# Down-weight quantization, low products and residual add moved in a fused cross-attention and FP4 feed-forward kernel

## The reference

```python
def fp4_quant_dequant(x):                 # along the last dim, blocks of 16
    scale = max(max(|xb|) / 6.0, 1e-12)
    q = GRID[searchsorted(MID, |xb / scale|)] * sign(xb) * scale
def fp4_linear(x, w):
    return einsum('bsk,nk->bsn', fp4_quant_dequant(x), fp4_quant_dequant(w))

x = x + autocorrelation_attention(layernorm(x), ctx, ctx, Wq, bq, Wout, bout)
h = silu(fp4_linear(layernorm(x), w_gate)) * fp4_linear(layernorm(x), w_up)   # 704 wide
x = x + fp4_linear(h, w_down)
```

## Time and profile before

| | |
|---|---|
| median of three executions | 526.64 us |
| profiled execution | 528.21 us, its span 526.4 us |
| busy, share of the span | TensorE 91%, VectorE 87%, ScalarE 74%, GpSimd 48% |
| mean granted TensorE clock | 0.964 |
| mean duration, split h (L533, L534, L536) | 1.2 to 1.3 us over all forms |
| largest_h (L1182), scaling_h (L1176) | 1620 ns, 1698 ns |
| ScalarE's copy of a weight fill, gate and up | four in 2.87 us |
| hqT transposes, issue to landing | 3.8 us median |

### The profile page before, as it was taken

One profiled execution on the slowest core, in us unless ns is written; L12 is line 12 of the kernel. 1 busy time (PEld: TensorE's weight loads), 2 busy tenths in 40 slices (PEclk: granted clock), 3 DMA queues, 4 the chain that ended last, 5 costly groups with the idle time before them and its releaser, 6 DMA issues.

```text
span 526.4 us, 10114 instructions
## 1 busy us (share of the span) xinstructions
PE 476.7 (91%) x3490; PEld 315.4 (60%) x3490; DVE 456.9 (87%) x762; ACT 391.9 (74%) x670; POOL 254.2 (48%) x326
## 2 busy tenths in 40 slices
PE   4599897858699999999999999999999999899957
PEld 4587787723355666666656666666666666466635
DVE  3789967598679999999999999999999999999981
ACT  3267875775978888888888788888888877766661
POOL 3225550256245566665655556666565558333330
PEclk9989997978899999999999999999999999899989
DMA  8988810432055676576675575656666564444636
GB/s 274 346 264 269 277 51 26 86 85 56 1 95 106 134 131 129 120 132 128 143 125 116 121 140 122 130 116 126 141 121 138 117 118 93 97 97 95 133 69 150
DMA packets 164723, 68.68 MB, mean 130 GB/s; under 512 B 129088, under 2 KB 164416, under 8 KB 164672
## 3 DMA queue, kind: packets, MB, share of 16 engines
q1 hardware_dynamic: 164672, 68.03, 57.3%
HBM read 27.38 MB, written 9.18 MB: 69 GB/s over the span
## 4 chain that ended last, share of the span: by engine, by line
issue 34%; POOL 21%; DVE 20%; PE 13%; ACT 5%; DMA 4%; SPq 1%; POOLq 1%; DVEq 1%; ACTq 0%
POOL ctx_sb L466 13%; POOL sl L482 6%; DVE w_q_lo L1144 4%; DVE ctx_sb L1097 3%; DVE y_h L1176 2%; DVE x_t L895 2%; PE ps L724 2%; ACT h_c L536 2%; PE ps L842 2%; ACT h_c L533 2%; PE ps L843 1%; DMA w_raw<-in_L_ffn_w_up_dram 1%; PE ps L704 1%; PE ps L844 1%; PE ps L714 1%
## 5 line engine op out<-in xcount | busy, mean ns | idle before, releaser
L842 PE MATMUL ps<-guT_hi,a_xT 128*128 128x512 f16 (+1 forms) x384 | 141.9, 370 | 14.1 <-DVE hb L1092 7.4
L843 PE MATMUL ps<-guT_lo,a_xT 128*128 128x512 f16 (+1 forms) x384 | 142.1, 370 | 0.0
L844 PE MATMUL ps<-guT_hi,a_xT 128*128 128x512 f16 (+1 forms) x384 | 141.6, 369 | 0.0
L852 PE MATMUL ps<-dT_hi,hqT 128*128 128x256 f16 x704 | 130.5, 274 | 7.6 <-ACT a_xT L594 5.7
L466 POOL TENSOR_TENSOR ctx_sb<-w_q_lo,sl 128x704 f16<-128x704 f16 x62 | 96.2, 1574 | 29.4 <-DVE ctx_sb L1097 29.3
L533 ACT ACTIVATE h_c<-y_h 128x1408 bf16<-128x1408 bf16 (+3 forms) x39 | 47.8, 1226 | 75.9 <-DVE y_h L1176 58.7
L854 PE MATMUL ps<-dT_lo,hqT 128*128 128x256 f16 x384 | 88.4, 275 | 0.0
L517 POOL TENSOR_TENSOR xs<-xs,w_raw 128x512 f32<-128x512 f32 x30 | 36.0, 1200 | 101.1 <-issue 101.1
L852 PEld LDWEIGHTS ps<-dT_hi,hqT 128*128 128x128 f16 x704 | 69.3, 98 | 18.7 <-issue 6.0
L842 PEld LDWEIGHTS ps<-guT_hi,a_xT 128*128 128x128 f16 x384 | 38.1, 99 | 62.5 <-issue 15.7
L844 PEld LDWEIGHTS ps<-guT_hi,a_xT 128*128 128x128 f16 x384 | 38.2, 100 | 40.5 <-issue 3.5
(11 more groups left out here) (161 smaller groups left out, 863.9 us busy)
## 6 DMA issues: line engine op xcount, KB each, us to landing
xs<-in_x_dram SPq DMA_DIRECT2D x16, 512.0 KB, 6.1
ctx_sb<-in_ctx_dram SPq DMA_DIRECT2D x16, 512.0 KB, 5.1
out_dram<-a_xT SPq DMA_DIRECT2D x64, 128.0 KB, 2.0
w_raw<-a_scratch SPq DMA_DIRECT2D x60, 128.5 KB, 2.7
hqT<-ctx_sb SPq DMA_TRANSPOSE x64, 3.8
w_raw<-in_L_ffn_w_down_dram SPq DMA_DIRECT2D x1, 704.0 KB, 6.3
w_raw<-in_L_ffn_w_gate_dram SPq DMA_DIRECT2D x1, 640.0 KB, 5.9
w_raw<-in_L_ffn_w_up_dram SPq DMA_DIRECT2D x1, 640.0 KB, 6.9
```

The source lines that it names most:

```text
L842: pe.matmul(dst, xt[:, c, :], guT[0][:, c, n0:n1], start=(c == 0), stop=False)
L843: pe.matmul(dst, xt[:, c, :], guT[1][:, c, n0:n1], start=False, stop=False)
L844: last = pe.matmul(dst, xt[:, KC + c, :], guT[0][:, c, n0:n1], start=False, stop=(c == KC - 1))
L852: pe.matmul(dst, hqT[:, j % 4, c, :], dT_hi[:, c, :], start=(c == 0), stop=False)
```

## The change

Four things are edited, in the order of the kernel:
- **Weights.** The load of the down weights goes ahead of the last two quads. `w_prepare(1)` runs in quad 14, its maximum is spread between the last correlations, scales and both segments follow the last evac_qk; both `w_finish` go between the softmax's sum and `wp`. ScalarE splits them before the exponential and evacuates all eight gate and up fills after it. The low part of the gate and up weights is written one quad later and waits for the next segment's w_finish. The transposes of the down weights go ahead of the filler products (28 in place of 20) and between tiles of pairs 0 and 1.
- **Stages 0 and 1.** In stage 0 ScalarE does silu(0) first; from stage 1 on (before, from stage 2) VectorE does the x steps among the h steps.
- **Low products.** GpSimd does low_scales ahead of low_h, and low_h waits for scaling_h (`yh_done`). Those of pairs 29 and 30 are done by VectorE, in one instruction each.
- **Residual.** L855 and ScalarE's copy go. VectorE computes bank x inv_out + xs for both tiles of a pair in one instruction, after products_x, and SP stores a pair at once. The last pair's tiles are done singly.
- **Drain** (st = NP): the order of VectorE's steps, and of SP's stores and transposes, is new.

```diff
@@ SP @@
             for i in range(2, NQ):
+                if i == NQ - 2:
+                    down_v = w_raw[:, 256 * GU_CH:WCOLS].rearrange("p (c n) -> p c n", n=FF)
+                    sp.dma_start(down_v, w_down.rearrange("(c p) n -> p c n", p=P)).then_inc(s["d_loaded"], 16)
                 load_x(i)
                 load_c(i)
...
-                    sp.wait_ge(s["loh"], i + 1)
+                    if i // 2 >= NP - 3:
+                        sp.wait_ge(s["z_lo"], i // 2 - NP + 4)
+                    else:
+                        sp.wait_ge(s["loh"], i + 1)
...
+            def store(q):
+                sp.wait_ge(s["o_done"], q + 1)
+                sp.dma_start(out[2 * q:2 * q + 2].rearrange("b l d -> l b d"), of[:, 2 * (q % 2):2 * (q % 2) + 2, :]
+                             ).then_inc(stored[q % 2], 16)
...
-                if tile_ok(2 * st - 8):
-                    store(2 * st - 8)
                 if pair_ok(st + 1):
                     turn_x(st + 1)
-                if tile_ok(2 * st - 7):
-                    store(2 * st - 7)
+                if pair_ok(st - 4) and st < NP:
+                    store(st - 4)
+                if st == NP + 1:
+                    store(NP - 4)
+                    turn_h(2 * NP - 2)
+                    store(NP - 3)
+                    turn_h(2 * NP - 1)
+                    store(NP - 2)
+                    store_last(0)
+                    store_last(1)
@@ GpSimd @@
             def w_lo(g):
                 pool.wait_ge(s["w_hi"], g + 1)
+                if g + 1 < N_GU:
+                    pool.wait_ge(s["w_steps"], finish_at(g + 1) + 3)
...
-                if turn(i - 2) is not None:
-                    w_lo(turn(i - 2))
+                if turn(i - 3) is not None:
+                    w_lo(turn(i - 3))
...
+            w_lo(N_GU)
+            w_lo(N_GU + 1)
...
             for st in range(FIRST, END):
                 if st == NP:
                     low_scales(NP - 1)
-                if pair_ok(st - 3) and st <= NP + 1:
-                    low_h(st - 3)
                 if 2 <= st < NP:
                     low_scales(st - 1)
+                if pair_ok(st - 3) and st < NP:
+                    pool.wait_ge(s["yh_done"], st - 1)
+                    low_h(st - 3)
@@ ScalarE @@
             keep_v(NQ // QT - 1)
-            evacuate_weights(act, range(EARLY))
+            w_split(N_GU)
+            w_split(N_GU + 1)
             act.wait_ge(s["t_steps"], 3)
             act.activation(wexp[:, :], corr[:, 0, 0:P], ACT.Exp, bias=nmx[:, 0:1]).then_inc(s["t_exp"], 1)
-            evacuate_weights(act, range(EARLY, GU_FILLS))
-            w_split(N_GU)
-            w_split(N_GU + 1)
+            evacuate_weights(act, range(GU_FILLS))
+            w_hi(N_GU)
+            w_hi(N_GU + 1)
...
+                    if st >= -2:
+                        evacuate_weights(act, range(GU_FILLS + 2 + st, GU_FILLS + 3 + st))
+                elif st == 0:
+                    silu(0)
+                    normalise_x(st + 3)
+                    square_x(st + 4)
+                    scale_high(st)
+                    silu(1)
+                    split_x(n)
+                    evacuate_weights(act, range(GU_FILLS + 2, GU_FILLS + 3))
@@ TensorE @@
-        EARLY, GU_FILLS = 5, 2 * 2 * KC
+        EARLY, GU_FILLS = 4, 2 * 2 * KC
...
+            spread_largest(1, bank(4)[:, 3 * P:4 * P])
             correlate(NQ - 1)
...
-                pe.matmul(dst, ident_out[:, :], xs[:, j, :], start=False, stop=True).then_inc(s["d_done"], 1)
+                last.then_inc(s["d_done"], 1)
...
-            for _ in range(20):
-                pe.matmul(bank(6)[:, 0:P], ones[:, :], ident[:, :], start=True, stop=True)
+            pe.wait_ge(s["w_lo"], len(SEGS))
+            for f in range(GU_FILLS, GU_FILLS + 2):
+                transpose_weights(f)
+            for _ in range(28):
+                pe.matmul(bank(4)[:, 0:P], ones[:, :], ident[:, :], start=True, stop=True)
@@ VectorE @@
+            def low_h(p):
+                dve.wait_ge(s["sl"], p + 2 - SC0)
+                times_runs(hq[:, p % 2, :, FF:2 * FF], h_g, sl[:, (p + 1) % 2, 0:2 * RUN_H], RUN_H).then_inc(s["z_lo"], 1)
+
+            def residual(q):
+                dve.wait_ge(s["d_done"], 2 * q + 2)
+                need(dve, stored[q % 2], 16 * (q // 2))
+                dve.scalar_tensor_tensor(out=of[:, 2 * (q % 2):2 * (q % 2) + 2, :], in0=ps[:, 6:8, 0:D], scalar=inv_out[:, 0:1],
+                                         in1=xs[:, 2 * q:2 * q + 2, :], op0=ALU.mult, op1=ALU.add).then_inc(s["o_done"], 1)
...
                     if st >= 1 and pair_ok(xa):
                         products_x(xa)
+                    if pair_ok(st - 4):
+                        residual(st - 4)
                     if scaled(st):
                         dve.wait_ge(sc, 2 * (st - SC0) + 2)
                     if pair_ok(j):
                         scaling_h(j)
+                    if st == NP - 1:
+                        high_h(p)
+                        low_h(p)
...
                 if st == NP:
                     gate_up(2 * j)
                     last_scale(0)
+                    last_y(0)
+                    residual(NP - 4)
                     offset_h(p)
-                    last_y(0)
+                    grid_h(p)
+                    high_h(p)
+                    low_h(p)
                     gate_up(2 * j + 1)
                     last_scale(1)
                     last_y(1)
-                    grid_h(p)
-                    high_h(p)
+                    residual(NP - 3)
                     last_grid(0)
                     last_grid(1)
-                if st in (-1, 0):
-                    w_finish(N_GU + 1 + st)
+                    residual(NP - 2)
+                    residual_last(0)
+                    residual_last(1)
```

127 lines of the change are left out of this document (51 added, 76 removed).

## The result

The changed kernel takes 518.64 us, median of four executions (518.27 to 519.56); the kernel before, run beside it, 527.21 (526.01 to 527.96). The ratio is 0.9842, with a 95% interval of 0.9817 to 0.9868. The profiled execution took 519.56, its span is 517.8 us, its mean granted clock 0.974.

The account below looks back on a forecast made before the run. Bound: a loop of VectorE from scales to scaling_x (6.11 us), then GpSimd's add, low products and low scales (5.83), 11.94 a stage. Opening -11.5, middle +11.5, drain -8.5 sum to -8.5: from median 526.64 to 518 us, range 512 to 527.

Parts of the forecast that it names:

- Part 1, the residual: Steady stages: the residual on VectorE, inside the loop with no cover, adds 0.65 us a stage; TensorE's 11.8 becomes 10.9.
- Part 2, the order: Steady stages: low scales ahead of low products bring -0.16 us; with the residual stage 12.43, +11.5 over 23 stages.
- Part 3, the drain: From stage 27 on: low products no longer beside products_x -4.7, shorter end -3.8; together -8.5 us, bounds -6.5 and -11.
- Part 4, the opening: Start to grid_h of stage 4: rearranged weights, fillers and first stages gain -11.5 us, bounds -5 and -13.
- (a): Attention phase: GpSimd's low part moves away from w_finish's last product, -1.5 us, bounds 0 and -3.
- (b): Before the first gate product: later ScalarE fill copies and eight filler products cost +1.0 us, bounds +0.5 and +3.
- (c): First pair after the fillers: 7.1 us instead of about 10 at half clock; second gate_up ends at 118.9.
- (d): Steps after the second gate_up: offset_h of stage 2 at 130.0 instead of 138.85, -8.9 us.
- (e): Two more stages, to grid_h of stage 4: 23.6 us instead of 26.25, -2.6.
- Lock lost: Rival, steady stages: second low product begins after offset_h is asked for; +0.67 a stage, 533.5 us; chance 0.12.
- TensorE's clock: Rival, steady stages: 1.5 us idle a stage brings half clock, +2.5, 520.5 us; chance 0.10.
- A free residual: Rival, steady stages: the residual fills an idle VectorE slot, the loop stays as cheap, 507 us; chance 0.03.

Follow-up runs that it names:

- res_early: Changed kernel with VectorE's residual moved from behind products_x to ahead of offset_h: 502.40 us, ratio 0.9508.
- res_tensor: Changed kernel with the residual's fp32 product back on TensorE and ScalarE copying a pair: 504.16 us, ratio 0.9550.
- end_fill: Changed kernel plus 15 filler products ahead of the down products of tile 60: 516.96 us, ratio 0.9807.
- old_w_lo: Changed kernel with the low part of the gate and up weights back beside w_finish: 520.02 us, ratio 0.9862.
- no_early_fill: Changed kernel without the eight filler products ahead of the product with Wout: 518.59 us, ratio 0.9846.
- no_late_fill: Changed kernel without the 28 filler products ahead of the first gate product: 520.59 us, ratio 0.9876.
- no_yh_wait: Changed kernel without the wait of GpSimd's low products for scaling_h: 526.36 us, ratio 0.9975.
- scales_gap_again: Second run of scales_gap, unchanged, beside a variant without early fillers: 494.07 us, ratio 0.9364.
- scales_gap: res_early with GpSimd's low scales done in the same stage, after grid_x, beside VectorE's reciprocal: 493.41 us, ratio 0.9349.

## Why the prediction was right, step by step

The forecast was 518 us, measured are 518.64; faster was the likeliest case and is what came. The three stretches of the table are each within 0.4 us, but not all of what stands in them was right, and so close a sum is in part luck.

- **Part 1, the residual.** Taken at 0.65, its step is 0.66 (270.07 to 270.73), its duration 0.74, the upper one of the two readings. It was placed inside the loop at full cost, and res_early shows just that, as do the two stages of 11.8 that the changed kernel runs before its first residual. TensorE's stage of 11.8 with it is shown by res_tensor; without it, TensorE is busy 88.68 of 100 us, which is 11.05 of a stage of 12.46 against the 10.9 estimated.
- **Part 2, the order.** -0.16 was forecast, -0.144 measured. Stage 12.43 forecast, 12.461 measured. Low scales, low products and offset_h stand as laid out: the scales free of a meeting, offset_h 1.90 long (2.0 forecast), no wait before the scales.
- **Part 3, the drain.** -8.5 forecast, -8.36 measured, and here two errors cancel. The stages saved 5.6 (from 51.55 to 45.92 over four) where 4.7 was taken: the term of 0.5 for low scales that meet something was charged to all four, 2.0 in all, while it measures 1.24: nothing in stage 27, 0.45 in stages 28 and 29 (offset_x 0.86), 0.34 in stage 30 (grid_x 0.75). The last two stages are also shorter than the 12.0 and 13.14 that the forecast set for them, but on both sides (11.45 and 11.14, before 12.71 and 12.57). The part behind gate_up of tile 62 went from 28.56 to 25.93, -2.6 instead of -3.8. That time, +25.93, lies at the half-clock end of the two values that the prediction gave, 24.3 and 25.8, and I had taken 24.8, between them. end_fill shows the cause for 0.7 of the 1.2 us missing. The rest is the last tile's transposition: in end_fill, where the last tile waits for it, it is issued 16.5 after gate_up of tile 62 (506.59, 490.11) and takes 3.9, where 16 and 3.6 were taken. That VectorE's low_h for pairs 29 and 30 is what shortened this part was argued from the order of the instructions; no run puts it back on GpSimd.
- **Part 4, the opening.** -11.5 forecast, -11.87 measured. (a) The correlation came 1.8 earlier in the profiled executions (87.38 to 85.59); 1.5 was taken. old_w_lo bears out the sign alone; its profile still shows 1.4 of the 1.8 with the meeting back, so the cause of this gain stays open. (b) The chain from the exponential to the product with Wout grew by 1.48, to the first gate product by 1.41 (22.74 to 24.15); +1.0 was taken, within its bounds. no_early_fill shows the fillers as the cause up to Wout only: without them the gate product comes later still (24.87). The first gate product came at 110.58, forecast 110.5. (c) It ran at full clock; the second gate_up ended at 119.11, forecast 118.9, and no_late_fill prices the fillers at 2.5. (d) offset_h of stage 2 at 129.63, forecast 130.0. (e) From grid_h of stage 2 to that of stage 4 are 23.60, forecast 23.6. Of the 8.8 us gained between the first gate product and grid_h of stage 2 (28.88 to 20.05), 2.5 are shown by a run; the rest is laid to the moved down weights and the new order of stages 0 and 1, which no run takes back. And the fit of the whole stretch to 0.4 us is luck in part: the profiled execution is one of the group at 130.5 to 130.6; the other group would have made it -13.6 to -14.0 (grid_h of stage 4 at 152.51 in end_fill, 152.17 in no_yh_wait), outside the bound of -13.
- **Lock lost** did not happen: the second low product starts near 276.46 (two in 3.01 from 274.96), 0.37 before offset_h is asked for, and the low scales took 0.65 and not 1.30. The margin of 0.38 that the rival turned on was right; it is thin. No run lost it in a steady stage, so the price of the loss stays an estimate.
- **TensorE's clock** did not fall in the middle: 1.00 from 200 to 300 us with TensorE idle 11 us of them, the last stretch of each stage behind the residual's wait, which the waits list as 38.9 us over 28 times. The rival did not come true for a loop with one idle stretch of 1.4 us a round. The Trainium skill (TensorE: Matmul & The Clock Gate, HAM oscillation — how this bites in real kernels) tells of a loop that waits about 3 to 5 us for a DMA in every round; the waits here are shorter, so the case that the Trainium skill tells of was not tested here, and the prediction took it for nearer than it is. Single stretches show both: half clock behind 3.80 us of idle (0.50 from 503 to 509) and behind 8.84 (0.72 from 110 to 117 in no_late_fill); behind about 2.5 us ahead of the first gate product full clock in most executions (2.54 in the changed kernel), and half clock 1.3 us later in one (2.56 in scales_gap_again).
- **A free residual** was given 0.03, rightly for this kernel. But what would have made it free was one line away, and the prediction, which had the loop and its two halves worked out, asked only what the residual costs in its place. It would have been a sentence: behind scaling_x, VectorE waits for GpSimd in any case.

So the change is a sum of a cost in each stage and of two gains at the ends, -20.2 and +11.6. The cost is neither the residual's work nor a worse balance of engines, but its place. With that one call moved the same change gives 502.40, 4.9% under before, and with the low scales moved off the loop as well 493.41, 6.5% under.

Open stays why executions of one opening reach the correlation over 1.7 us (83.9 to 85.6). The clock from 16 to 32 us differs with it, 0.89 in those up to 84.65 and 0.79 to 0.87 in most of the later ones (of two at 84.77, one has 0.89 and one 0.79); which comes first was not tried. Behind the correlation the difference grows to 2 us by the clock from 86 to 92 us: 0.50 in the three executions that reach grid_h of stage 2 at 130.5 to 130.6 (the changed kernel, res_early, scales_gap), 0.65 to 0.71 in the five at 128.5 to 128.9. (The fourth at 130.5, scales_gap_again, had 0.70 there and lost its time behind the first gate product.)
